# Attention's output projection in three products of high and low parts, with the context split by VectorE

## The chip, the cores and the metric

The kernel runs on one core of a Trainium2 chip. The metric is the device time of one execution in microseconds (us). The engines are TensorE (PE, with its weight loads as PEld), VectorE (DVE), ScalarE (ACT), GpSimd (POOL) and SyncE (SP), which here issues most of the DMAs.

## The reference, cut to what matters

The input is x of 2 x 2048 tokens with 256 features. Three residual steps follow each other:

```
x = x + 0.5 * ffn(layernorm(x))      # 8 experts, the best 2 per token, hidden width 176
x = x + attn(layernorm(x))
x = x + 0.5 * ffn(layernorm(x))      # the same expert weights
```

In attn a causal convolution of 3 taps makes q, k and v of 64 features each. The tokens are cut into 32 blocks of 128, 8 heads attend causally within each block, and the context ends in two products:

```
mha_out = einsum('bqhk,hko->bqo', ctx, wo) + bo     # 64 features
out = mha_out @ proj_w + proj_b                     # 64 -> 256 features
```

Everything is float32. The change touches only the last product.

## The kernel before, in words

The tokens are 32 tiles of 128 rows. The kernel has a first expert stage, the attention stage and a second expert stage; each engine's program is written out by hand in the same turns, and semaphores alone connect them.

The attention stage runs in turns i, one per tile (`turns`, from -8 to 36), as a software pipeline. In turn i TensorE does, in this order: the convolution of a pair of tiles, q and k in odd turns (L1602, 18 matmuls) and v in even turns (L1611, 12); the scores of tile i (L1618 and L1623); the transposes of tile i-1's probabilities (L1629); the transposes of a later tile's input and of an earlier tile's output (L1637, L1648); the router's logits (L1664); the **projection** of tile i-2 (`project`, L1590, into bank G); the context of tile i-1, already multiplied with wo (L1679, into bank F); the per-head q and k of tile i+1 (L1689); and the values of tile i (L1699, into bank F too). Since L1699 overwrites what L1679 left in F, it waits until VectorE has copied it: `after(pe, t["mhaT"], i)`.

VectorE's turn i has, around the change: the maxima of the scores (L1311), in even turns the low part of v (L1315), the residual addition of the projection's result (L1327, waits for `out`), its statistics (L1330, L1333), the copy of the logits (L1261), the **copy of the context** with its bias from F into mhaT (L1342, waits for `mha`, signals `mhaT`), the low part of a later tile's input (L1274), the sum of the experts' rows for a later tile (L968, twice), the reciprocals of the exponentials' sums (L1353), and the copy of q and k (L1266), for which the next turn's scores wait. After L1353 GpSimd multiplies the probabilities (L683) and then issues its gathers (L691) and scatters (L700), which are indirect DMAs. ScalarE copies the transposed probabilities (L804), and computes the exponentials (L813).

mhaT and proj_sb are float32. 64 features fill only half of the 128 partitions; with heads of even and odd number in the two halves, proj_w stands in both halves, and the product adds them. The expert stages and the convolution use float32r operands instead: a value is kept as a high part, rounded when it is written, and a low part, the difference, and three products (high by high, high by low, low by high) replace one float32 product.

proj_w is loaded by SyncE with the small constants, in `loads`.

Of the kernel before, what the change touches and what calls it, by code (L numbers as in the profile page):

```python
# [15 lines left out]
ALU = mybir.AluOpType  # L16
ACT = mybir.ActivationFunctionType
AX = mybir.AxisListType
F32 = mybir.dt.float32
F32R = mybir.dt.float32r  # L20
# [4 lines left out]
P = 128  # L25
BATCH, SEQ, D = 2, 2048, 256
TOKENS = BATCH * SEQ
TILES = TOKENS // P
DC = D // P
# [14 lines left out]
TAPS, W = 3, 64  # L44
# [52 lines left out]
def macaron_kernel(nc, x, conv_w, conv_b, wq, wk, wvT, wo, bq, bk, bo, proj_w, proj_b, gupT, dpT, rwT,  # L97
                   out, h_dram, y_dram):
    ctx = ExitStack()
    with ctx:  # L100
        def sb(name, shape, dt=F32):
            return ctx.enter_context(nc.sbuf_tensor(name, shape, dt))
# [28 lines left out]
        wo_sb = sb("wo_sb", [KD, NH, W])  # L131
# [3 lines left out]
        bo_sb = sb("bo_sb", [W, 1])  # L135
        cbv_sb = sb("cbv_sb", [W + 1, 1])
        wvo_sum = sb("wvo_sum", [W + 1, W])
        mha_bias = sb("mha_bias", [P, 1])
        proj_sb = sb("proj_sb", [P, D])
        projb_sb = sb("projb_sb", [33, D])  # L140
        projb_parts = sb("projb_parts", [P, D], F32R)
        ones_r = sb("ones_r", [P, P], F32R)
# [4 lines left out]
        minus_ident = sb("minus_ident", [P, P], F32R)  # L147
# [111 lines left out]
        G_USED = LG_AT + (POST + 2) * E  # L259
# [7 lines left out]
        prec = sb("prec", [P, 2, NH])  # L267
        mhaT = tile_oh[:, :, :].rearrange("p j n -> p (j n)").bitcast(F32)[:, 2 * P:3 * P]
        eps = sb("eps", [P, 1])
# [12 lines left out]
        F = pb("F", 1)  # L282
# [51 lines left out]
        def logits_of(t):  # L334
# [14 lines left out]
                 (bqk_sb[:, 1, :], bk.rearrange("a (m p) -> p (a m)", p=P)), (wvT_sb[:, :, :], wvT),  # L349
                 (wo_sb[:, :, :], wo), (bo_sb[:, :], bo), (proj_sb[0:W, :], proj_w), (proj_sb[W:2 * W, :], proj_w),  # L350
                 (projb_sb[0:1, :], proj_b), (projb_sb[32:33, :], proj_b)]
# [89 lines left out]
        def turns(turn):  # L441
            for i in range(FIRST_TURN, LAST_TURN):
                turn(i)
# [40 lines left out]
        def _(sp):  # L484
# [82 lines left out]
            sp.wait_ge(first["tokens"], 1)  # L567
            sp.dma_start(conv_sb, conv_w).then_inc(loaded, 16)
            store_y(0)
            fill_pads()  # L570
# [149 lines left out]
        def _(a):  # L720
# [42 lines left out]
            def attention():  # L763
# [71 lines left out]
                a.preload_act_table_set("natural_log_exp_and_others")  # L835
                a.wait_ge(loaded, 16 * (len(loads) + 1))
                a.activation(conv_qk[0][:, :, :], conv_sb_qk, ACT.Copy).then_inc(wprep, 1)
                for c in range(DC):
                    a.activation(conv_v_parts[0][:, c, :, :], conv_sb_v[:, c, :, :], ACT.Copy).then_inc(wprep, 1)
                a.activation(projb_all[:, D:], zeros[:, 0:G_USED - D], ACT.Copy)  # L840
                a.wait_ge(projb, 4)
                a.activation(projb_all[:, 0:D], G[:, 0:D], ACT.Copy).then_inc(projb, 1)
                a.wait_ge(projb, PROJB_AT)
# [88 lines left out]
        def _(v):  # L932
# [260 lines left out]
            def attention():  # L1193
# [93 lines left out]
                def turn(i):  # L1287
# [52 lines left out]
                    if there(i - 1):  # L1340
                        v.wait_ge(t["mha"], i)
                        v.tensor_tensor(mhaT[:, :], F[:, 0:P], mha_bias[:, 0:1].to_broadcast([P, P]), ALU.add  # L1342
                                        ).then_inc(t["mhaT"], 1)
                    if there(i + 3) and i >= 0:
# [50 lines left out]
                for c in range(DC):  # L1395
                    v.tensor_tensor(conv_v_parts[1][:, c, :, :], conv_sb_v[:, c, :, :],
                                    conv_v_parts[0][:, c, :, :].bitcast(F32), ALU.subtract).then_inc(wprep, 1)
                turns(turn)

# [9 lines left out]
        def _(pe):  # L1409
# [173 lines left out]
            def attention():  # L1583
# [4 lines left out]
                def project(b):  # L1588
                    pe.wait_ge(t["mhaT"], b + 1)
                    pe.matmul(G[:, 0:D], mhaT[:, :], proj_sb[:, :], start=False, stop=True, skip_group_check=True  # L1590
                              ).then_inc(t["out"], 1)

# [162 lines left out]
            keep_clock(F[:, :], 44)  # L1755
            pe.wait_ge(wprep, 7 + 2 * (1 + DC))
            attention()
# [46 lines left out]
```

## Time and profile before

| what | value |
|---|---|
| median of 3 runs (lowest, highest) | 794.87 us (792.56, 800.15) |
| the profiled execution: its own time | 796.36 us |
| its span, first to last instruction | 794.6 us |
| mean granted TensorE clock | 0.961 of full |
| busy: PE, PEld | 690.0 us (87%), 603.7 us |
| busy: DVE, ACT, POOL | 528.2 us (66%), 490.2 us (62%), 335.8 us (42%) |
| attention's tiles: context copies L1342, first to last start | 272.0 to 575.7 us, 32 of them |

The busy shares are means over stages with different limits. The expert stages, 605 to 750 us among them, keep TensorE almost wholly busy; within the attention stage this holds for some turns and not for others, so that stage has to be read turn by turn. A matmul's end is modelled by the profile: two matmuls overlap in the rows, and what one of them costs is the distance between starts.

### The profile page before, as it was taken

The numbers are of one execution on the slowest core, as the hardware profiler recorded it, in microseconds if no ns is written. First come the engines' busy times: TensorE is split into PE (matmuls) and PEld (weight loads), VectorE is DVE, ScalarE is ACT, GpSimd is POOL, SyncE is SP. The second block draws the span as 40 slices with busy tenths as digits, with TensorE's granted clock in tenths as the row PEclk, the third lists the DMA queues.
The fourth block names the chain that finished last, engine by engine and source line by source line (L and its number), as shares of the span: only waits on it lengthen the run. The fifth ranks groups of instructions, "written<-read, shape, count | busy, mean of one in ns | idle before, by whom it ended". The sixth has DMA issues, their size and how long they took to land. (4 is left out here: it accounts for less than half of the span.)

```text
span 794.6 us, 19426 instructions
## 1 busy us (share of the span) xinstructions
PE 690.0 (87%) x5468; PEld 603.7 (76%) x5468; DVE 528.2 (66%) x1813; ACT 490.2 (62%) x1734; POOL 335.8 (42%) x361
## 2 busy tenths in 40 slices
PE   3999799999999799998988889989635999999944
PEld 3976699999975688877767777778424999999833
DVE  6578566666656587786767576857664777777643
ACT  4766566666653587767766657767522666666633
POOL 5100544444416444455555545252551444444500
PEclk9999999999999999999999999999956999999979
DMA  9930354444422110011111111010124444444279
GB/s 313 279 110 13 124 147 141 143 130 127 128 82 85 39 41 28 28 41 55 55 55 48 61 41 48 22 55 2 61 91 117 132 128 125 128 131 126 83 288 346
DMA packets 57863, 83.40 MB, mean 105 GB/s; under 512 B 9520, under 2 KB 43827, under 8 KB 57780
## 3 DMA queue, kind: packets, MB, share of 16 engines
q1 hardware_dynamic: 44772, 47.63, 19.0%
q0 software_dynamic: 13008, 34.69, 14.0%
q8 instruction: 49, 0.80, 0.4%
q14 instruction: 34, 0.28, 0.1%
HBM read 45.77 MB, written 37.44 MB: 105 GB/s over the span
## 5 line engine op out<-in xcount | busy, mean ns | idle before, releaser
L1539 PE MATMUL CC<-w_hi,turned_parts 128*128 x568 | 172.5, 345 | 0.3 <-DVE turned_parts L1161 0.2
L655 POOL DMA_INDIRECT shared<-h_rows,tok_i x71 | 67.3, 948 | 119.0 <-issue 58.7
L667 POOL DMA_INDIRECT y_rows<-shared,y_dest x71 | 69.9, 985 | 88.7 <-DVE y_dest L1173 74.9
L683 POOL TENSOR_TENSOR pr<-pr,prec 128x1024 f32<-128x1024 f32 x31 | 58.8, 1895 | 112.2 <-DVE prec L1353 110.9
L1539 PEld LDWEIGHTS CC<-w_hi,turned_parts 128*128 128x128 f32 x568 | 103.8, 190 | 1.0 <-issue 0.9
L1539 PE MATMUL CC<-w_lo,turned_parts 128*128 x284 | 91.8, 323 | 0.0
L729 ACT ACTIVATE shared<-CC 128x176 f32<-128x176 f32 x142 | 45.1, 317 | 75.1 <-PE CC L1539 72.6
L813 ACT ACTIVATE pr<-SS,nmax 128x128 f32<-128x128 f32 x256 | 90.4, 400 | 0.8 <-issue 0.8
L700 POOL DMA_INDIRECT h_regions<-h_store,dest x64 | 63.1, 987 | 47.3 <-DVE dest L1256 27.3
L1156 DVE TENSOR_TENSOR shared<-shared,CC 128x176 f32<-128x176 f32 x142 | 48.0, 338 | 51.6 <-ACT shared L729 30.0
L691 POOL DMA_INDIRECT yg<-y_rows,slot_i x64 | 62.6, 977 | 34.9 <-DMA y_rows<-shared 15.5
L745 ACT ACTIVATE shared<-SS 128x256 f32<-128x256 f32 x142 | 54.6, 385 | 26.5 <-issue 15.5
L804 ACT ACTIVATE shared<-CC 128x512 f32<-128x512 f32 x64 | 34.7, 594 | 48.1 <-PE CC L1629 45.2
L813 ACT ACTIVATION_READ_ACCUMULATOR pr<-SS,nmax 128x1 f32 x256 | 61.8, 241 | 0.0
L1539 PEld LDWEIGHTS CC<-w_lo,turned_parts 128*128 128x128 f32 x284 | 54.1, 191 | 0.0
L1556 PE MATMUL SS<-w_hi,turned_parts 128*128 x142 | 51.8, 364 | 1.3 <-DVE turned_parts L1167 1.0
L1161 DVE TENSOR_TENSOR turned_parts<-A,turned_parts 128x256 fp32r<-128x256 f32 x72 | 30.6, 425 | 29.5 <-ACT turned_parts L734 28.5
L1311 DVE TENSOR_REDUCE nmax<-SS 128x8 f32<-128x1024 f32 x32 | 39.1, 1221 | 13.4 <-PE SS L1623 10.4
L1623 PEld LDWEIGHTS SS<-shared 64*128 64x128 f32 x512 | 31.1, 187 | 18.0 <-issue 9.7
L1161 DVE TENSOR_TENSOR turned_parts<-B,turned_parts 128x256 fp32r<-128x256 f32 x70 | 29.8, 425 | 21.0 <-ACT turned_parts L734 16.8
L1526 PE MATMUL A<-ident,shared 128*128 128x128 f32 x144 | 29.0, 283 | 16.1 <-DMA shared<-h_regions 12.6
L781 ACT ACTIVATE lnvar<-moments,eps 128x2 f32<-128x2 f32 x39 | 11.7, 300 | 48.9 <-DVE moments L1367 48.0
(318 smaller groups left out, 2055.4 us busy)
## 6 DMA issues: line engine op xcount, KB each, us to landing
shared<-h_regions SPq DMA_DIRECT2D x71, 129.0 KB
y_rows<-shared SPq DMA_DIRECT2D x71, 128.0 KB
w_lo<-y_rows SPq DMA_DIRECT2D x9, 512.0 KB, 8.4
x_sb<-in_x_dram SPq DMA_DIRECT2D x8, 512.0 KB, 8.3
out_dram<-x_sb SPq DMA_DIRECT2D x16, 256.0 KB, 5.7
w_hi<-y_rows SPq DMA_DIRECT2D x7, 512.0 KB, 11.9
w_lo<-in_gupT_dram SPq DMA_DIRECT2D x2, 1408.0 KB, 10.7
h_regions<-pad_rows SPq DMA_DIRECT2D x15, 129.0 KB
```

The source lines that it names most:

```text
L655: pool.indirect_dma_start(out=rows[:, s % RING, 0:D], out_offset=None, in_=h_dram[:, :], in_offset=bass.IndirectOffsetOnAxis(ap=tok_i[:, s ...
L667: pool.indirect_dma_start(out=y_dram[0:TOPK * TOKENS, :], out_offset=bass.IndirectOffsetOnAxis(ap=y_dest[:, s:s + 1], axis=0), in_=y_sb[:, ...
L683: pool.tensor_tensor(pr[:, q, :, :], pr[:, q, :, :], prec[:, q, :].unsqueeze(2).to_broadcast([P, NH, P]), ALU.mult).then_inc(t["norm"], 1)
L691: pool.indirect_dma_start(out=yg[:, q, k, :], out_offset=None, in_=y_dram[:, :], in_offset=bass.IndirectOffsetOnAxis(ap=slot_i[:, b, k:k + ...
L700: pool.indirect_dma_start(out=h_regions[:, :], out_offset=bass.IndirectOffsetOnAxis(ap=dest[:, q, k:k + 1], axis=0), in_=hr[:, q, :], in_o ...
L729: a.activation(gate[:, p, :], CC[:, 512 * p:512 * p + H], ACT.Silu).then_inc(r["silu"], 1)
L745: a.activation(y_sb[:, u % RING, :], SS[:, 512 * (u % 2):512 * (u % 2) + D], ACT.Copy).then_inc(r["y_sb"], 1)
L813: e = a.activation(pr[:, u % 2, h, :], SS[:, h * P:(h + 1) * P], ACT.Exp, bias=nmax[:, u % 2, h:h + 1], accum_out=psums[:, u % 2, h:h + 1])
L1156: v.tensor_tensor(hid[:, p, 0:H], gate[:, p, :], CC[:, 512 * p + H:512 * p + GU], ALU.mult).then_inc(r["hid"], 1)
L1161: v.tensor_tensor(rowsT_lo[:, p, :], (A, B)[p][:, 0:D], rowsT_hi[:, p, :].bitcast(F32), ALU.subtract).then_inc(r["rowsT_lo"], 1)
L1539: i = pe.matmul(CC[:, 512 * (u % 2):512 * (u % 2) + GU], rows_part[:, u % 2, c * P:(c + 1) * P], weights, start=(n == 1), stop=(n == 3 * DC))
L1556: pe.matmul(acc, hidA_hi[:, u % 2, :], w_hi[:, at_a], start=True, stop=False)
```

## The change

The context of a tile is written by VectorE twice: the high part (the sum of F and the bias, rounded to float32r) and then, after a wait for it, the low part (the same sum less the high part), which now gives the signal `mhaT`. They lie in two tiles that are no longer used by then. proj_w is split likewise, once: ScalarE writes the high part, VectorE the low part, between the first expert stage and the attention's turns. `project` becomes three float32r matmuls of 256 columns. proj_w's two loads move from `loads` to behind the load of the convolution's weights, in SyncE's queue.

```diff
-        proj_sb = sb("proj_sb", [P, D])
+        proj_lo = sb("proj_lo", [P, D], F32R)
...
-        mhaT = tile_oh[:, :, :].rearrange("p j n -> p (j n)").bitcast(F32)[:, 2 * P:3 * P]
+        mhaT_hi, mhaT_lo, proj_hi = minus_ident, ones_r, projb_parts
+        proj_sb = tile_oh[:, :, :].rearrange("p j n -> p (j n)").bitcast(F32)[:, 1536 + G_USED:1536 + G_USED + D]
...
-                 (wo_sb[:, :, :], wo), (bo_sb[:, :], bo), (proj_sb[0:W, :], proj_w), (proj_sb[W:2 * W, :], proj_w),
+                 (wo_sb[:, :, :], wo), (bo_sb[:, :], bo),
...
             sp.dma_start(conv_sb, conv_w).then_inc(loaded, 16)
+            for half in range(2):
+                sp.dma_start(proj_sb[W * half:W * (half + 1), :], proj_w).then_inc(loaded, 16)
             store_y(0)
...
-                a.wait_ge(loaded, 16 * (len(loads) + 1))
+                a.wait_ge(loaded, 16 * (len(loads) + 3))
...
                 a.wait_ge(projb, 4)
+                a.activation(proj_hi[:, :], proj_sb[:, :], ACT.Copy).then_inc(wprep, 1)
...
-                        v.tensor_tensor(mhaT[:, :], F[:, 0:P], mha_bias[:, 0:1].to_broadcast([P, P]), ALU.add
-                                        ).then_inc(t["mhaT"], 1)
+                        step(v.tensor_tensor(mhaT_hi[:, :], F[:, 0:P], mha_bias[:, 0:1].to_broadcast([P, P]), ALU.add))
+                        v.scalar_tensor_tensor(out=mhaT_lo[:, :], in0=F[:, 0:P], scalar=mha_bias[:, 0:1],
+                                               in1=mhaT_hi[:, :].bitcast(F32), op0=ALU.add, op1=ALU.subtract
+                                               ).then_inc(t["mhaT"], 1)
...
+                v.wait_ge(wprep, 7 + 2 * (1 + DC) + 1)
+                v.tensor_tensor(proj_lo[:, :], proj_sb[:, :], proj_hi[:, :].bitcast(F32), ALU.subtract
+                                ).then_inc(wprep, 1)
...
-                    pe.matmul(G[:, 0:D], mhaT[:, :], proj_sb[:, :], start=False, stop=True, skip_group_check=True
-                              ).then_inc(t["out"], 1)
+                    for n, (part, weights) in enumerate(((mhaT_hi, proj_hi), (mhaT_hi, proj_lo), (mhaT_lo, proj_hi))):
+                        x = pe.matmul(G[:, 0:D], part[:, :], weights[:, :], start=False, stop=(n == 2),
+                                      skip_group_check=True)
+                    x.then_inc(t["out"], 1)
...
-            pe.wait_ge(wprep, 7 + 2 * (1 + DC))
+            pe.wait_ge(wprep, 7 + 2 * (1 + DC) + 2)
```

VectorE's queue in an even turn of the attention stage, before (tile_oh holds mhaT) and then in the changed kernel (minus_ident and ones_r now hold the two parts):

```order
L1261 TENSOR_TENSOR lg<-G,zeros 128x8
L1342 TENSOR_TENSOR tile_oh<-F,mha_bias 128x128
L1274 TENSOR_TENSOR turned_parts<-A,turned_parts 128x2x128
L968 SCALAR_TENSOR_TENSOR x_sb<-yg,wts,x_sb 128x256 x2
L1353 RECIPROCAL prec<-psums 128x8
L1266 TENSOR_TENSOR shared<-CC,bqk_sb 128x1024
```

```order
L1265 TENSOR_TENSOR lg<-G,zeros 128x8
L1346 TENSOR_TENSOR minus_ident<-F,mha_bias 128x128
L1347 SCALAR_TENSOR_TENSOR ones_r<-F,mha_bias,minus_ident 128x128
L1278 TENSOR_TENSOR turned_parts<-A,turned_parts 128x2x128
L972 SCALAR_TENSOR_TENSOR x_sb<-yg,wts,x_sb 128x256 x2
L1359 RECIPROCAL prec<-psums 128x8
```

One instruction is new between the first write of the context and all that follows; nothing else changes its place.

## Rows read from the trace of the kernel before

**Rows 1.** Busy time by stretch: us, sums of each engine, PEclk, DMA share, GB/s.

```profile
275.00:300.00 25.00, 24.71 (x247) 20.51 (x246) 20.04 (x57) 19.76 (x77) 12.18 (x10) 1.00 0.12 33
400.00:450.00 50.00, 42.27 (x397) 35.29 (x398) 33.52 (x108) 33.23 (x129) 26.65 (x23) 0.97 0.15 49
```

**Rows 2.** Waits, 272 to 579 us: who waited for whom, us, times, longest.

```profile
DVE x_sb L1327 <- remote: 19.5, 9, 3.2
PE F L1699 <- issue: 16.9, 14, 5.1
...
DVE x_sb L1327 <- PE G L1590: 10.9, 11, 2.6
```

**Rows 3.** Timeline, a turn in which TensorE waits for the copy.

```profile
456.96 0.28 DVE L1342 TENSOR_TENSOR tile_oh<-F,mha_bias 128x128 f32<-128x128 f32 x1
...
457.34 0.47 PE L1699 MATMUL F<-wvo_hi,vst_hi 128*128 128x512 f32 x1 [1.05 <-issue]
```

**Rows 4.** Timeline, 441 to 445 us: projection, GpSimd's indirect DMAs, residual addition.

```profile
441.35 0.68 PE L1590 MATMUL G<-proj_sb,tile_oh 128*128 128x256 f32 x2
...
442.62 0.99 POOL L700 DMA_INDIRECT h_regions<-h_store,dest  x1 [0.30 <-issue]
...
444.51 0.42 DVE L1327 TENSOR_TENSOR x_sb<-x_sb,G 128x256 f32<-128x256 f32 x1 [3.14 <-remote]
```

**Rows 5.** Timeline, TensorE, a turn without idle time: start, us, instruction.

```profile
432.32 0.68 PE L1590 MATMUL G<-proj_sb,tile_oh 128*128 128x256 f32 x2
432.93 1.09 PE L1679 MATMUL F<-shared 128*64 128x128 f32 x16
```

**Rows 6.** Timeline, TensorE, the convolution's 18 matmuls: first, last, and what follows.

```profile
458.11 0.28 PE L1602 MATMUL B<-turned_parts,conv_qk_hi 128*128 128x256 f32 x1
...
460.13 0.28 PE L1602 MATMUL B<-turned_parts,conv_qk_hi 128*128 128x256 f32 x1
460.25 0.60 PE L1618 MATMUL SS<-mask_bf,ident_bf 128*128 128x512 bf16 x2
```

**Rows 7.** Groups by shape: xcount, busy us, mean ns, idle before.

```profile
L968 DVE SCALAR_TENSOR_TENSOR x_sb<-yg,wts,x_sb 128x256 f32<-128x256 f32 x44 | 21.2, 481 | 0.8
...
L1342 DVE TENSOR_TENSOR tile_oh<-F,mha_bias 128x128 f32<-128x128 f32 x26 | 7.4, 283 | 1.5 <-remote 1.2 <-PE F L1679 0.2
```

**Rows 8.** Instructions on bank G, one line: ns min/median/max, starts, shapes.

```profile
L1166 DVE TENSOR_TENSOR turned_parts<-G,turned_parts x70: 284/292/294, 89.9 to 751.5; 128x128 fp32r<-128x128 f32 x70
```

**Rows 9.** Timeline, VectorE: two instructions, the second waiting for the first.

```profile
319.32 0.16 DVE L1301 SCALAR_TENSOR_TENSOR at<-moments,at 128x2 f32<-128x2 f32 x1
319.51 0.16 DVE L1304 SCALAR_TENSOR_TENSOR arstd<-at,arstd 128x2 f32<-128x2 f32 x1
```

**Rows 10.** Timeline, VectorE, 313 to 315 us; a turn of TensorE without idle time.

```profile
313.34 0.42 DVE L1327 TENSOR_TENSOR x_sb<-x_sb,G 128x256 f32<-128x256 f32 x1 [0.50 <-PE G L1590]
313.91 0.43 DVE L1330 BATCH_NORM_STATS2 astats<-x_sb 128x6 f32<-128x256 f32 x1
...
314.63 0.28 DVE L1342 TENSOR_TENSOR tile_oh<-F,mha_bias 128x128 f32<-128x128 f32 x1
314.82 0.41 DVE L1274 TENSOR_TENSOR turned_parts<-A,turned_parts 128x256 fp32r<-128x256 f32 x1
```

**Rows 11.** Timeline, TensorE, 315 us: the values start after the context copy.

```profile
315.06 0.50 PE L1699 MATMUL F<-wvo_hi,vst_hi 128*128 128x512 f32 x1
```

**Rows 12.** Timeline, both engines, a turn with time to spare.

```profile
322.44 1.10 PE L1679 MATMUL F<-shared 128*64 128x128 f32 x16 [0.38 <-issue]
324.56 0.50 PE L1699 MATMUL F<-wvo_hi,vst_hi 128*128 128x512 f32 x1
...
323.58 0.29 DVE L1342 TENSOR_TENSOR tile_oh<-F,mha_bias 128x128 f32<-128x128 f32 x1
```

**Rows 13.** Timeline before the turns: a ScalarE copy; VectorE's last weight part, first wait.

```profile
235.00 0.36 ACT L842 ACTIVATE tile_oh<-G 128x256 f32<-128x256 f32 x1
...
235.84 0.62 DVE L1396 TENSOR_TENSOR conv_v<-tile_oh,conv_v 128x192 fp32r<-128x192 f32 x2
...
239.12 1.00 DVE L968 SCALAR_TENSOR_TENSOR x_sb<-yg,wts,x_sb 128x256 f32<-128x256 f32 x2 [2.66 <-DMA yg<-y_rows,slot_i]
```

**Rows 14.** Busy time by stretch, two drops of the granted clock; columns as rows 1.

```profile
446.40:449.90 3.50, 3.50 (x15) 3.17 (x14) 2.70 (x7) 1.08 (x3) 1.98 (x2) 0.51 0.02 5
470.30:473.80 3.50, 3.50 (x19) 2.73 (x16) 2.37 (x8) 2.15 (x7) 2.99 (x3) 0.51 0.00 0
```

**Rows 15.** Line L1342: count, ns min/median/max, first and last start.

```profile
L1342 DVE TENSOR_TENSOR tile_oh<-F,mha_bias x32: 257/281/292, 272.0 to 575.7; 128x128 f32<-128x128 f32 x32
```

## The prediction

> **What bounds the kernel now.** The expert stages keep TensorE busy and the change does not touch them, so I read the attention stage. First the busy time by stretch [rows 1]: early in the stage TensorE is busy 24.71 of 25.00 us, while between 400 and 450 us it is busy 42.27 of 50. In the early turns TensorE is the limit; later something else sets the pace, and VectorE (33.5 of 50) is not full either. So there a chain of waits is the limit. The list of waits [rows 2] names a link of it: 14 times TensorE stands idle in front of L1699, 16.9 us in sum. L1699 overwrites bank F and waits for the context copy L1342. The timeline of such a turn shows the link: L1342 starts at 456.96 and takes 0.28, TensorE's L1699 starts at 457.34, 0.10 us after the copy's end, and it had been idle for 1.05 us [rows 3]. The copy itself is late because the residual addition L1327 in front of it was. In the turn around 442 us the projection starts at 441.35 and takes 0.68, but the addition that waits for it starts at 444.51; GpSimd is issuing indirect DMAs until 443.61 [rows 4]. Nine such waits, 19.5 us, have no releaser in the view ("remote"), against 10.9 us in 11 waits that end with the projection [rows 2]. So in the slow turns the signal of the projection comes late for a reason other than the length of its matmuls. My reading is that the chain goes: addition, context copy, values and convolution, scores, exponentials, reciprocals, GpSimd, its DMAs, and again the addition. The new VectorE instruction is put inside this chain; the shorter projection lies mostly outside.
>
> **Part 1: the projection on TensorE, shorter.** Before, its two float32 passes start at 432.32 and the next instruction, without idle time, at 432.93: 0.61 us [rows 5]. Float32r matmuls of the same 256 columns, weights changing each time, come at (460.25 - 458.11) / 18 = 0.119 us [rows 6]. Three cost 0.36, so each tile saves 0.25 us of TensorE, 31 tiles 7.8 us if all of it counted. The result's signal comes earlier by a little less; I take 0.17 (0.25 less the longer tail of three overlapping ends, an estimate). These are bounds too: three loads of weights that could not overlap would make the saving zero.
>
> The Trainium skill (FP8 and Floating Point Precision, "TensorE Precision Notes") says that a true FP32 product takes four passes through the array. By that, four against three of 0.119 would save only 0.12 us per tile; the trace does not agree, with 0.61 us for the float32 product, five times 0.119.
>
> **Part 2: the context copy on VectorE, longer.** The high part costs what the copy did, 0.283 [rows 7]; written as float32r it has the form of a subtraction from bank G, 0.292 at the median [rows 8], no difference worth a term. Then comes the wait: a waiting neighbour starts 0.19 to 0.20 us after a start of 0.16 [rows 9], so it costs 0.035. The low part is a scalar_tensor_tensor of 128 columns, a form with no row of its own. The same operation takes 0.481 for 256 columns [rows 7] and 0.16 for two [rows 9]; half way between is 0.32. Sum: `mhaT` comes 0.36 us later after the copy's start, and what follows on VectorE moves by as much, since L1274 starts 0.19 after L1342 now [rows 10] and would start 0.315 + 0.24 after it. Bounds: 0.28 (the TensorTensor of 128 columns, [rows 8], with the wait hidden) and 0.63 (0.481 for the operation, 0.15 for the wait, as between L1327, 0.42 long, and L1330, 0.57 later, [rows 10]). I take 0.36, nearest to the same operation's own rows. Queued behind it on VectorE are the low part of the next input, the experts' sums, the reciprocals (GpSimd waits for them) and L1266 (the next scores wait for it).
>
> The Trainium skill (VectorE: DVE Perf Modes, "The DRAIN you can't avoid") holds that a semaphore between two VectorE instructions costs nothing extra. By that the delay would be 0.32; here L1274 starts before L1342 has ended [rows 10], and the waiting pair has a gap [rows 9], so the wait has a price.
>
> **Part 3: what it does to the turns.** In the 14 turns where L1699 waits for the copy, the chain grows by 0.36: 14 x 0.36 = **+5.0 us**. TensorE's saving is worth nothing there: it only makes TensorE idle earlier. In 3 of these the addition waited visibly for the projection's end; 3 x 0.17 = **-0.5**. The other 17 turns are of two kinds. In the turn at 313 us the copy ends at 314.91 and L1699 starts at 315.06 [rows 10, 11]: with the 0.10 us that a signal takes, 0.05 is to spare. The later copy then takes TensorE's saving and 0.14 to 0.31 more; I take 0.2, for half of them: 8 x 0.2 = **+1.6**. In the turn at 323 us the copy ends at 323.87 and L1699 starts at 324.56, 0.59 to spare; but L1679 had waited 0.38 for ScalarE anyway [rows 12], so a shorter projection in front of it gains nothing: **0**, for the other nine. Sum **+6.1 us**.
>
> **Part 4: the rest.** ScalarE's high part of proj_w (0.36, as its copy of 256 columns) and VectorE's low part (0.42, as L1327) fall before the turns. VectorE ends its last weight part at 236.46 and then idles 2.66 us for a gather [rows 13]; if that cover were gone, they would cost 0.4 to 0.8 us, once. The two loads, 64 x 256 numbers each, pass in SyncE's queue in front of the first expert stage's stores, which wait for expert results anyway, and have that whole stage to land. Bank G, the tiles reused and the tail after the last turn: 0.
>
> **The sum.** 796.36 + 6.1 = 802.5 for the profiled execution, which lies 1.5 us over the median of the three runs. From the median, 794.87 + 6.1 = **801.0 us**, 0.8% slower. The bounds of the copy's price alone give 14 x 0.28 - 0.5 + 0.6 = +4 and 14 x 0.63 - 0.5 + 8 x 0.5 = +12.3, that is 799 to 807. A change of under 1% (7.9 us, 786.9 to 802.8) cannot be told from none with the spread of 7.6 us that three runs showed.
>
> **The rivals.**
> *The gain arrives (not slower).* TensorE is the limit where it is 99% busy [rows 1], and if the extra VectorE time falls into its waits for the projection (10.9 us in 11, [rows 2]), some 16 turns (half, an estimate: those without idle time in front of L1679) gain 0.25: 794.87 - 4 = 791; all 31 would give 787. For it: [rows 1, 5]. Against: in [rows 10, 11] the margin is 0.05 us, and the slow turns wait for exactly the instruction that grows. It decides where more than 0.2 us is to spare behind the copy. Chance 0.2.
> *VectorE binds in every turn (slower).* Everything behind the copy moves by 0.36, the q and k copy with it, for which the scores wait; then the turns with time to spare pay as well: 31 x 0.36 = +11.2, 806; at the upper price 814. For it: 33.5 of 50 us busy, and waits on both sides of the chain. Against: in [rows 12] the margin is 0.59. Chance 0.2.
> *More drops of the clock.* The granted clock fell to 0.51, its lower level of 1.2 GHz, for 3.4 us at 446 and at 470 us, each time after turns with idle time in front of L1699 [rows 14, 3]; TensorE does half its work there, so a drop costs at most 1.7 us. Two more, on top of my forecast: 804.4. Two fewer: 797.6. Chance of two more 0.1.
> The Trainium skill (TensorE: Matmul & The Clock Gate, "HAM oscillation") says that idle gaps make the clock fall again; the drops stand behind such gaps here, so the trace agrees.
> *It does not do what it says:* three float32r matmuls with their loads cost as much as the float32 pair. Then the nearly tight turns pay the full 0.36: +8 x 0.16 = 1.3 over the forecast, 802.3. Against: [rows 6]. Chance 0.05, counted with the forecast's range.
>
> **Chances.** Forecast 0.45, and 0.05 for the last rival; around 801 with a few us either way, two thirds of it is under 802.8. Gain 0.2: mostly within 1%, 0.05 beyond. VectorE in every turn 0.2 and clock 0.1: nearly all slower. Together: faster by over 1% 0.05, within 1% 0.52, slower by over 1% 0.43. The range takes the gain at its likely size and the slower rival at its lower price: 791 to 807.
>
> **What would show it.** Right: two rows for the context, 0.28 and about 0.32 us, starts 0.32 apart; L1699's counterpart starting about 0.7 after the first; three matmuls 0.12 apart; more than 14 waits and more than 16.9 us in front of the values. Wrong: the low part under 0.25 or above 0.45; TensorE's idle time in front of the values no larger, and the mean distance of two tiles, now (575.7 - 272.0) / 31 = 9.80 us [rows 15], shorter instead of 0.2 longer. What would overturn it all is a change of the lateness of projection signals, 19.5 us now [rows 2], since no part of my sum moves that.

## The result and the profile after

| | before | after |
|---|---|---|
| median of 4 runs (lowest, highest) | 796.73 us (792.56, 800.15) | 810.01 us (806.89, 813.68) |
| ratio of after to before, 95% interval | | 1.0149 [1.0106, 1.0193] |
| profiled execution: its time, span | 796.36, 794.6 us | 812.69, 811.0 us |
| mean granted TensorE clock | 0.961 | 0.936 |
| first to last context copy, per tile | 303.6 us, 9.80 us | 317.1 us, 10.23 us |

The kernel became 1.5% slower, twice what was forecast (0.8%), and the time lies above the range. In the two profiled spans the difference is 16.4 us: 13.4 between the first and the last context copy, 0.6 ahead of them (they start at 272.6 instead of 272.0 us) and 2.4 behind them. So the loss is in the attention turns, as forecast, 0.43 us for each of 31 tile distances instead of 0.2. In this pair of executions a good part of it can be the clock; see the end of this section. A few executions of some kernels fell in a much slower state of the chip (up to 3582 us); the ratios leave them out, while the medians of "split late" and "signal alone" on the slow chip hold two and one of them.

The context's two instructions in the profile after, by line (count, ns min/median/max, first and last start), answer to [rows 15]:

```profile
L1346 DVE TENSOR_TENSOR minus_ident<-F,mha_bias x32: 256/281/292, 272.6 to 589.7; 128x128 fp32r<-128x128 f32 x32
...
L1347 DVE SCALAR_TENSOR_TENSOR ones_r<-F,mha_bias,minus_ident x32: 350/351/352, 272.9 to 590.0; 128x128 fp32r<-128x128 f32 x32
```

The high part costs what the copy did, the low part 0.351 us where 0.32 was forecast. A turn in which TensorE waits for them, first VectorE's rows (start, us, instruction, idle time before it); the next row of the values is below. This answers to [rows 3]:

```profile
454.45 0.42 DVE L1331 TENSOR_TENSOR x_sb<-x_sb,G 128x256 f32<-128x256 f32 x1 [3.74 <-remote]
455.01 0.43 DVE L1334 BATCH_NORM_STATS2 astats<-x_sb 128x6 f32<-128x256 f32 x1
455.59 0.18 DVE L1337 BATCH_NORM_AGGREGATE moments<-astats 128x2 f32<-128x6 f32 x1
455.69 0.13 DVE L1265 TENSOR_TENSOR lg<-G,zeros 128x8 f32<-128x8 f32 x1
455.74 0.28 DVE L1346 TENSOR_TENSOR minus_ident<-F,mha_bias 128x128 fp32r<-128x128 f32 x1
456.05 0.35 DVE L1347 SCALAR_TENSOR_TENSOR ones_r<-F,mha_bias,minus_ident 128x128 fp32r<-128x128 f32 x1
456.32 0.41 DVE L1278 TENSOR_TENSOR turned_parts<-A,turned_parts 128x256 fp32r<-128x256 f32 x1
...
456.50 0.47 PE L1710 MATMUL F<-wvo_hi,vst_hi 128*128 128x512 f32 x1 [1.59 <-issue]
```

L1347 starts 0.31 after L1346, so the wait between them costs 0.03 as forecast. The values (L1710) start 0.76 after the high part, against 0.38 before [rows 3], and L1278 starts 0.58 after it, against 0.19 [rows 10]. Both the values and the queue are 0.38 to 0.39 us later, counted from the start of the first write.

The turn that was costed at nothing because 0.59 us was to spare [rows 12] looks like this in the profile after, TensorE and VectorE:

```profile
322.73 0.37 PE L1600 MATMUL G<-projb_parts,minus_ident 128*128 128x256 f32 x1
322.93 0.28 PE L1600 MATMUL G<-proj_lo,minus_ident 128*128 128x256 f32 x1
323.05 0.28 PE L1600 MATMUL G<-projb_parts,ones_r 128*128 128x256 f32 x1
323.26 1.09 PE L1690 MATMUL F<-shared 128*64 128x128 f32 x16
324.29 1.16 PE L1700 MATMUL CC<-tile_oh,wqk_sb 64*128 64x128 f32 x16
325.43 0.47 PE L1710 MATMUL F<-wvo_hi,vst_hi 128*128 128x512 f32 x1
...
324.66 0.28 DVE L1346 TENSOR_TENSOR minus_ident<-F,mha_bias 128x128 fp32r<-128x128 f32 x1
324.98 0.35 DVE L1347 SCALAR_TENSOR_TENSOR ones_r<-F,mha_bias,minus_ident 128x128 fp32r<-128x128 f32 x1
```

The low part ends at 325.33 and the values start at 325.43, the 0.10 us of a signal later: in this turn nothing is to spare any more, and the 0.38 that L1679 had waited for ScalarE is gone as well. The three products start 0.20, 0.12 and 0.21 us apart, 0.53 from the first to what follows, against 0.61 for the float32 pair [rows 5]. They save 0.08 us and not 0.25. Where float32r products follow each other the distance is 0.119 [rows 6]; here the first one, behind float32 matmuls, and the last one, before them, each take about 0.09 more.

The list of waits after, 272 to 592 us (who waited for whom, us, times, longest), answers to [rows 2]:

```profile
DVE x_sb L1331 <- remote: 27.0, 10, 3.7
...
PE F L1710 <- issue: 26.3, 22, 5.6
...
DVE x_sb L1331 <- PE G L1600: 6.8, 11, 1.2
```

TensorE now stands idle in front of the values 22 times for 26.3 us, where it was 14 times for 16.9. Taken turn by turn, the values start 0.10 us behind the end of the instruction that signals in 29 of 31 turns, before in 15. This counts the turns that the signal touches, not what they pay: on another chip, where the change costs only 0.39% (below), the same count is 29 against 7. The wait for the projection fell from 10.9 to 6.8 us, and the late signals ("remote") rose from 19.5 to 27.0. Busy times by stretch after (us, sums of PE, PEld, DVE, ACT, POOL, granted clock, DMA share, GB/s), two as in [rows 1] and the attention stage's core:

```profile
275.00:300.00 25.00, 24.03 (x246) 20.29 (x245) 20.27 (x58) 19.39 (x77) 11.49 (x9) 1.00 0.12 33
400.00:450.00 50.00, 44.36 (x397) 37.26 (x396) 34.14 (x111) 30.59 (x113) 26.46 (x24) 0.90 0.15 46
265.00:540.00 275.00, 244.72 (x2346) 206.66 (x2345) 195.84 (x624) 184.76 (x710) 135.84 (x113) 0.96 0.14 43
582.00:630.00 48.00, 22.84 (x109) 19.14 (x110) 25.75 (x132) 11.51 (x32) 15.31 (x16) 0.51 0.30 86
```

Early TensorE has become less busy, 24.03 of 25 instead of 24.71. In the core, VectorE is busy 195.84 of 275 us: 71%, still far from full.

The clock differs too. The span between the first and the last context copy, before and then after, and the stretch of the profile after in which the clock falls before the last copy:

```profile
272.00:575.70 303.70, 272.08 (x2608) 225.17 (x2608) 215.57 (x708) 209.35 (x806) 149.37 (x124) 0.98 0.13 42
```

```profile
272.60:589.70 317.10, 278.28 (x2639) 234.25 (x2639) 226.06 (x739) 210.44 (x808) 149.52 (x125) 0.95 0.13 40
580.90:589.70 8.80, 7.34 (x39) 6.13 (x39) 6.24 (x33) 3.87 (x10) 2.15 (x3) 0.50 0.05 17
```

By the clock's records TensorE is at its lower level (1.2 GHz) for 13.7 us of this span before and for 32.7 us after, and is busy for 13.7 and 30.4 of them. If it does half its work there, as the prediction has it, the 16.7 us more cost at most 8.4 of the 13.4 us.

### The profile page after: what moved, and what is told of

Same layout as the page of the kernel before. It is cut to its first block, busy times and chain, and to the rows that moved or that the text cites. A ratio compares the mean times of both kernels' runs of the same rounds, so it can differ in the third digit from the quotient of the medians.

```text
span 811.0 us, 19524 instructions
## 1 busy us (share of the span) xinstructions
PE 701.4 (86%) x5500; PEld 618.5 (76%) x5500; DVE 539.8 (67%) x1846; ACT 491.5 (61%) x1735; POOL 334.7 (41%) x361
## 3 DMA queue, kind: packets, MB, share of 16 engines
q0 software_dynamic: 13008, 34.69, 13.7%
## 4 chain that ended last, share of the span: by engine, by line
PE 75%; issue 8%; DVE 6%; DMA 5%; ACT 3%; SPq 2%; another core or an unknown queue 1%; POOL 1%; DVEq 0%; POOLq 0%; ACTq 0%
PE CC L1548 17%; PE CC L1640 4%; PE SS L1634 4%; PE CC L1700 4%; PE B L1613 4%; PE F L1710 4%; PE F L1690 3%; PE B L1622 3%; PE A L1535 2%; PE SS L1565 2%; PE SS L1566 2%; PE SS L1567 2%; PE SS L1568 2%; PE SS L1569 2%; PE B L1535 2%
## 5 line engine op out<-in xcount | busy, mean ns | idle before, releaser
L1548 PE MATMUL CC<-w_hi,turned_parts 128*128 x568 | 174.8, 349 | 0.2 <-DVE turned_parts L1165 0.2
L1700 PE MATMUL CC<-tile_oh,wqk_sb 64*128 64x128 f32 x512 | 41.5, 287 | 5.0 <-issue 4.6
L1535 PE MATMUL A<-ident,shared 128*128 128x128 f32 x144 | 29.3, 285 | 16.9 <-DMA shared<-h_regions 13.1
## 6 DMA issues: line engine op xcount, KB each, us to landing
w_hi<-y_rows SPq DMA_DIRECT2D x7, 512.0 KB, 12.1
```

Of the source, the lines that this page charges most:

```text
L1535: i = pe.transpose((A, B)[s % 2][:, c * P:(c + 1) * P], rows[:, s % RING, c * P:(c + 1) * P], ident[:, :])
L1548: i = pe.matmul(CC[:, 512 * (u % 2):512 * (u % 2) + GU], rows_part[:, u % 2, c * P:(c + 1) * P], weights, start=(n == 1), stop=(n == 3 * DC))
L1700: x = pe.matmul(CC[:, 512 * n + m * P:512 * n + (m + 1) * P], wqk_sb[W * n:W * (n + 1), m * P:(m + 1) * P], qk[W * n:W * (n + 1), q, :], s ...
```

## The experiments

All medians are of kernels timed in turns with the kernel before on the same chip. Two sorts of chip came up: on one the kernel before takes 797 us, on the other 758. I call them the slow and the fast chip; each sort came up on more than one chip. Short names in what follows: the **signal** is `mhaT`, for which TensorE waits; the **queue** is what stands behind the copy on VectorE. Letters in an expectation are explained in it or in the ones ahead of it.

| experiment | chip | median, us | before there | ratio [95%] | per tile, us |
|---|---|---|---|---|---|
| (before, profiled) | slow | | | | 9.80 |
| low part alone | slow | 805.89 | 797.45 | 1.0134 [1.0064, 1.0205] | 10.00 |
| products alone | slow | 799.05 | 797.45 | 1.0021 [0.9993, 1.0048] | 10.00 |
| low part twice | slow | 820.07 | 797.45 | 1.0284 [1.0229, 1.0339] | 10.52 |
| split late | slow | 804.06 | 797.45 | 1.0075 [1.0043, 1.0106] | 9.98 |
| signal alone | slow | 803.04 | 797.33 | 1.0080 [1.0054, 1.0106] | 9.96 |
| queue alone | slow | 801.76 | 797.33 | 1.0050 [1.0022, 1.0079] | 9.95 |
| copy first (before) | slow | 802.12 | 797.33 | 1.0058 [1.0027, 1.0089] | 9.81 |
| before again | fast | 758.60 | 758.74 | 0.9997 [0.9976, 1.0018] | 8.75 |
| after again | fast | 761.87 | 758.74 | 1.0039 [1.0022, 1.0056] | 8.85 |
| queue alone | fast | 761.74 | 758.74 | 1.0045 [1.0024, 1.0067] | 8.90 |
| signal alone | fast | 758.70 | 758.74 | 1.0002 [0.9988, 1.0017] | 8.77 |
| copy first (before) | fast | 761.53 | 757.71 | 1.0046 [1.0032, 1.0061] | 8.86 |
| copy first (after) | fast | 771.05 | 757.71 | 1.0159 [1.0132, 1.0186] | 9.10 |
| fillers (after) | fast | 769.41 | 757.71 | 1.0154 [1.0128, 1.0180] | 9.10 |
| split on GpSimd | fast | 763.04 | 757.71 | 1.0075 [1.0051, 1.0099] | 8.79 |

"Per tile" is from one profiled execution, first to last context copy by 31; the verdicts go by the ratios. The distances on the slow chip carry the clock with them. "Products alone" shows it: its ratio is 1.002, but the execution that was profiled is the slowest of its ten (803.75 us), with 10.00 us per tile. Between its first and last copy TensorE was at the lower clock for 28.7 us (before: 13.7) and busy for 26.7 of them, which would cost up to 6.5 us; its span there is 6.3 us longer than before's. So up to 0.2 us per tile can come without any change on VectorE.

**1. The low part alone, in the kernel before.** The same added instruction, written to a spare tile, gives the signal; the projection stays float32.

```diff
-v.tensor_tensor(mhaT, F, bias, add).then_inc(t["mhaT"], 1)
+step(v.tensor_tensor(mhaT, F, bias, add))
+v.scalar_tensor_tensor(out=ones_r, in0=F, scalar=bias, in1=mhaT, op0=add, op1=subtract).then_inc(t["mhaT"], 1)
```

> The kernel before (float32 projection, one copy used) with the change's low-part instruction added behind the context copy: it computes the low part into a spare tile, nobody reads it, and it alone gives the signal mhaT. Theory A (the signal mhaT comes 0.39 us later per tile and nearly every turn waits for it): 31 x 0.39 = 12 us over before plus about 1 for a slower clock, and within 3 us of the changed kernel, since the shorter projection was worth at most 31 x 0.08 = 2.5. Theory B (the float32r products of the change themselves cost time, in the array or by the clock): under 5 us over before. As predicted blind (14 turns pay 0.36): +5.

Measured 1.0134, against 1.0149 for the whole change. These ratios agree within their intervals (0.6 to 2.0% and 1.1 to 1.9%). The waits of its profiled execution, which at 802.45 us is one of the two short ones of four (median 805.89), 272 to 592 us:

```profile
PEld F L1701 <- issue: 29.5, 23, 5.7
PE F L1701 <- issue: 24.4, 21, 5.5
DVE x_sb L1327 <- PE G L1592: 17.8, 18, 2.3
...
DVE x_sb L1327 <- remote: 9.9, 5, 3.7
```

The 21 waits and 24.4 us in front of the values are those of the profile after (22 and 26.3). "Remote" is at 9.9 us, half of before's 19.5. The profile puts such a wait sometimes to a late signal and sometimes to the projection, so the two lines are to be read together: 30.4 us before, 27.7 here, 33.8 after. The waits of the addition thus do not grow with the added instruction alone.

**2. The products alone.** The change with one copy only: the low part of the context is left out, and the third product takes the high part a second time.

```diff
-step(v.tensor_tensor(mhaT_hi, F, bias, add))
-v.scalar_tensor_tensor(out=mhaT_lo, ...).then_inc(t["mhaT"], 1)
+v.tensor_tensor(mhaT_hi, F, bias, add).then_inc(t["mhaT"], 1)
...
-for ... in enumerate(((mhaT_hi, proj_hi), (mhaT_hi, proj_lo), (mhaT_lo, proj_hi))):
+for ... in enumerate(((mhaT_hi, proj_hi), (mhaT_hi, proj_lo), (mhaT_hi, proj_hi))):
```

> The changed kernel with one copy of the context only: the low part of the context is left out, and the third product uses the high part again, so TensorE's work is that of the change and VectorE's that of before (this kernel leaves the context's low part out of the result). Theory A: VectorE's queue is as before, so the time is too; TensorE saves 0.08 us a tile by the rows of the changed kernel, worth 0 to 2.5 us: between 3 us under before and before. Theory B: 5 us or more over before. My blind figure of 0.25 us per tile would show as 4 to 8 us under before.

Measured 1.0021, with 1 inside the interval. The products gain nothing in time: at 0.08 us per tile they could give 31 x 0.08 = 2.5 us (0.3%) at most, and at the 0.25 of the forecast 7.8 us; the interval (-0.6 to +3.8 us) excludes both in full. The granted clock of these ten runs was lower than that of the kernel before beside them (medians 0.948 and 0.955), so a small gain may lie under it; this was not separated.

**3. The low part twice.** In the change the low part is computed a second time before the signal.

```diff
+step(v.scalar_tensor_tensor(out=mhaT_lo, in0=F, scalar=bias, in1=mhaT_hi, op0=add, op1=subtract))
 v.scalar_tensor_tensor(out=mhaT_lo, ...).then_inc(t["mhaT"], 1)
```

> The changed kernel with the low part computed twice in a row, the second giving the signal: another 0.385 us per turn between the copy's start and mhaT. Theory A: all turns but one or two pay it already, so 31 x 0.385 = 12 us over the changed kernel, 24 to 26 over before; the mean distance of two tiles grows by 0.385. If the changed kernel's extra time came from more drops of the clock, not from the delay itself: under 5 us over the changed kernel.

Measured 1.0284. Over the change this is 1.35% more, 10.8 us by the ratios or 0.35 us for each of 31 distances; the second low part with its wait is 0.351 + 0.035 = 0.39 long. The first one cost 0.34 per distance (10.7 us by experiment 1). The intervals are wide: 0.17 to 0.53 us for either. In the profiled executions the span between first and last copy grows by 9.1 us over the change's, 0.29 per distance, at much the same time at the lower clock (34.1 and 32.7 us). So the second low part is paid in most turns; for the first one no pair of executions at the same clock is on record.

**4. The split late.** VectorE copies the context in float32 and frees F, as before; the high and the low part are made from that copy at the end of the turn.

```diff
+v.tensor_tensor(mhaT, F, bias, add).then_inc(low_act, 1)
...
+step(v.tensor_copy(mhaT_hi, mhaT))
+v.tensor_tensor(mhaT_lo, mhaT, mhaT_hi, subtract).then_inc(t["mhaT"], 1)
```

> The changed kernel with the context copied once in float32, which alone releases bank F, and split from that copy into high and low part on VectorE at the end of the turn, behind the statistics (two instructions, some 0.5 us, and one copy more than the change). Theory A1 (what costs is the lateness of the signal that releases bank F): the signal comes as early as before, so within 3 us of before, although VectorE works more than in the changed kernel. Theory A2 (what costs is VectorE's time, wherever it stands in the turn, since its queue closes the loop): 31 x 0.5 = 15 us over before. Halfway, 5 to 8 over, if the turns with idle time on VectorE absorb it and the others do not.

Measured 1.0075. Between first and last copy its profiled execution is 5.7 us longer than before's, with about the same time at the lower clock (15.0 and 13.7 us). VectorE's rows of this kernel, grouped by shape:

```profile
L1375 DVE CAST minus_ident<-tile_oh 128x128 fp32r<-128x128 f32 x32 | 14.3, 446 | 0.0
L1376 DVE TENSOR_TENSOR ones_r<-tile_oh,minus_ident 128x128 fp32r<-128x128 f32 x32 | 11.0, 344 | 1.1
```

VectorE does 0.79 us more per turn here, twice the change's addition, at about half the change's cost by the ratios. So it is not VectorE's sum of work alone that counts but where in the turn it lies. It is still slower than before.

**5 and 6. Signal and queue apart.** The added instruction delays two things at once. "Queue alone" puts an instruction of its kind behind the signal, in the kernel before. "Signal alone" gives the signal by a write of one column (0.06 us) behind the next VectorE instruction, so the queue hardly grows.

```diff
 v.tensor_tensor(mhaT, F, bias, add).then_inc(t["mhaT"], 1)
+v.wait_ge(t["mhaT"], i)                                       # queue alone
+v.scalar_tensor_tensor(out=ones_r, in0=mhaT, scalar=bias, in1=mhaT, op0=add, op1=subtract)
```

```diff
-v.tensor_tensor(mhaT, F, bias, add).then_inc(t["mhaT"], 1)    # signal alone
+v.tensor_tensor(mhaT, F, bias, add)
 ...low part of the next input...
+v.memset(number_off[:, 0:1], 0.0).then_inc(t["mhaT"], 1)
```

Both were run on the fast chip first, beside the two kernels unchanged:

> The kernel before, unchanged, to have its profile from the same chip as the next three: the last four kernels ran on a chip where the kernel before takes 758 us, 40 us less than on the chip of its own profile. If this chip is the fast one, TensorE is busy over 97% of the attention stage and waits for the context copy in under 7 turns.

> The changed kernel, unchanged. Ratio to before 1.015 as on the first chip; with fillers it was 1.0154 on the second, so if fillers neither help nor cost, the same here. If the copy's place in TensorE's wait is all that matters, a chip without late signals would show under 1.008.

> The kernel before with a scalar_tensor_tensor of 128 columns behind the context copy, on the copy in SBUF: the signal mhaT is given first, as before, and only what follows on VectorE comes some 0.4 us later. Theory A (the signal is what costs): within 2 us of before. Theory C (VectorE's queue closes the loop): 8 to 12 us over, as much as with the low part alone. Half of each: 4 to 7.

> The kernel before with the signal mhaT given by a one-element memset behind the next VectorE instruction, so that it comes some 0.35 us later while VectorE's queue grows by 0.06 us only. Theory A: 8 to 12 us over before on a chip with late signals of TensorE, 3 to 8 on one without. Theory C: within 2 us of before.

There the whole change costs only 0.39%, which is 3.0 us or 0.10 us per tile out of 0.39 added; the longer queue costs as much (0.45%), and the late signal nothing (0.02%). The clock hardly enters here: between the first and the last copy it is at the lower level for 3.4 us in both profiles. Then on the slow chip:

> The same kernel as the one with VectorE's queue alone made longer, on another chip if the draw gives one. If this is a chip with late signals of TensorE (kernel before near 797 us): theory D (there the loop runs through VectorE, GpSimd and the late signals, and every instruction in VectorE's queue lies in it) expects 7 to 12 us over before; theory A (only the signal mhaT counts) within 2 us. On a chip without them (near 758): 3 us, as measured.

> The same kernel as the one with the signal alone late, on another chip if the draw gives one. On a chip with late signals: theory D expects 0 to 4 us over before, for the turns in which the values wait; theory A 8 to 12. On one without: 0, as measured.

Here the late signal costs 0.80% (0.54 to 1.06) and the longer queue 0.50% (0.22 to 0.79), so which of the two costs more is not settled. Their sum, 1.3%, fits the low part alone (1.34%, 0.64 to 2.05), but the intervals leave room. That the late signal costs time here and none on the fast chip is clear of the noise. VectorE and TensorE in one turn of "signal alone" on the slow chip:

```profile
333.22 0.28 DVE L1350 TENSOR_TENSOR tile_oh<-F,mha_bias 128x128 f32<-128x128 f32 x1
333.41 0.41 DVE L1274 TENSOR_TENSOR turned_parts<-A,turned_parts 128x256 fp32r<-128x256 f32 x1
333.78 0.06 DVE L1283 MEMSET number_off<- 128x1 f32 x1
...
333.95 0.47 PE L1708 MATMUL F<-wvo_hi,vst_hi 128*128 128x512 f32 x1 [0.23 <-issue]
```

The values start 0.73 after the copy instead of 0.38, while L1274 keeps its distance of 0.19: the edit moved the signal and left the queue, as it should. The waits of "signal alone" and then "queue alone" on the slow chip, 265 to 590 us:

```profile
PE F L1708 <- issue: 25.5, 21, 5.2
```

```profile
PE F L1702 <- issue: 19.7, 16, 5.2
```

The late signal brings the number of waits to that of the change (21 against 22); the longer queue leaves it near that of before (16 against 14) and costs through what is behind it instead.

**7. The context copied first.** The copy, or both parts, is put right behind the residual addition, ahead of its statistics and the copy of the logits.

```diff
 v.sem_inc(t["res"], 1)
+if there(i - 1):
+    v.wait_ge(t["mha"], i)
+    ...the copy, or both parts, with the signal...
 st.did(v.bn_stats(astats[:, 1, :], x_tile(b)))
```

> The kernel before with one instruction moved: the context copy stands directly behind the residual addition, ahead of the statistics and the copy of the logits. Theory A (the wait of L1699 for the copy sets the pace of the slow turns): the signal comes up to 0.7 us earlier there (1.28 us between the starts of addition and copy now, 0.55 then); TensorE's wait in front of L1699 in the 14 turns, 16.9 us without its share of the last turn 11.8, shrinks by up to 0.7 each: 4 to 8 us under before. Theory C (VectorE's queue as a whole closes the loop, and no single signal does): within 2 us of before.

> The changed kernel with both parts of the context made directly behind the residual addition. Theory A: the signal comes 0.7 us earlier, more than the 0.39 the change added: at or under before (-4 to +2 us), that is 10 to 16 us under the changed kernel. Theory C: VectorE's 0.385 us per turn stay in its queue: 5 to 8 us under the changed kernel at most, still over before.

> The kernel before with the context copy directly behind the residual addition, on another chip if the draw gives one. On a chip with late signals: theory A expects 4 to 8 us under before, since the signal comes 0.7 us earlier; theory D from 2 under to 4 over, as VectorE's queue keeps its length and what follows the copy waits for the context. On one without: 3.5 over, as measured.

Slower on both sorts of chip in the kernel before (0.46%, 0.58%), and 1.59% over before with both parts, on a fast chip where the change itself costs 0.39%. On the slow chip the one profiled execution shows no longer distance of tiles (9.81 us against 9.80), so where its 0.58% lies is not shown. A reason that fits is that an earlier place in the queue is not an earlier start: on the slow chip the copy now waits itself for TensorE's context, and holds up the statistics and the logits behind it (265 to 590 us):

```profile
DVE tile_oh L1332 <- PE F L1681: 9.7, 16, 1.1
```

**8. Fillers against the clock's drops.** Three idle matmuls of 512 bfloat16 columns before the wait for the signal, in the change.

```diff
+for _ in range(3):
+    pe.matmul(B, ident_bf, mask_4, start=True, stop=True)
 after(pe, t["mhaT"], i)
```

> The changed kernel with three filler matmuls of 512 bf16 columns (0.21 us each, results not used) into bank B, ahead of the wait for mhaT, so that TensorE is busy where it stood idle. If drops of the granted clock carry the extra time (changed kernel: seven drops between 265 and 580 us, 24 us at half clock, before: four): the clock holds and the time falls by 3 to 6 us. Theory A: the fillers lie in idle time of 0.5 to 1.7 us in most turns and cost up to 0.6 us in the tight ones: 0 to 5 us over the changed kernel, whatever the clock does.

Inconclusive: the run fell on a fast chip, where TensorE is nearly always busy, and the kernel with fillers is 1.5% over before where the change alone is 0.4%, so the fillers cost about 1.1%. It says nothing on the slow chip's clock, where the question arose; this test was not run there.

**9. The split on GpSimd.** VectorE makes one float32 copy and GpSimd the two parts.

```diff
+v.tensor_tensor(mhaT, F, bias, add).then_inc(low_act, 1)
...
+steps.did(pool.tensor_copy(mhaT_hi, mhaT))
+pool.tensor_tensor(mhaT_lo, mhaT, mhaT_hi, subtract).then_inc(t["mhaT"], 1)
```

> The changed kernel with VectorE's part as before (one float32 copy, which releases bank F), and both parts made from it by GpSimd, ahead of its wait for the reciprocals, where it idles 4 us a turn. Signal and VectorE's queue are as before, the three products as in the change: by theory A and C alike within 2 us of the kernel with the products alone, 797 to 800. If GpSimd's additional time pushes its gathers: up to 10 us over before.

Measured 1.0075 on a fast chip, where the change costs 0.39%. It is no cure. The two instructions take 294 and 490 ns at the median, in front of the multiplication of the probabilities; that this is what costs is argued, not shown. No version beat the kernel before on either chip, so none is proposed.

## Why the prediction was wrong

**The place held.** The added VectorE instruction between the context and its signal makes the kernel slower (experiment 1 alone gives 1.34 of 1.49%), the products bring nothing measurable (experiment 2), and all else (proj_w's parts, the loads, bank G) shows at most the 0.6 us by which the turns start later.

**Part 1, mis-sized.** The projection saves 0.08 us and not 0.25. The row at [rows 6] was measured within a run of float32r matmuls, and here three of them stand between float32 ones. The last rival, that it does not do what it says, was two thirds true. This moved the sum little: the -0.5 did not come, and that is all that Part 1 gave to it.

**Part 2, nearly right.** 0.39 us instead of 0.36: 0.351 for the low part, 0.035 for the wait. In 14 turns that is +0.4.

**Part 3, the first step that failed.** It let 14 turns pay in full, 8 pay 0.2, and 9 nothing, because in a turn like [rows 12] 0.59 us was to spare. It read the slack of one turn as if that turn stood alone. In the profile after, the same turn has nothing to spare, and the values wait for the signal in 29 of 31 turns. The explanation offered is that the turns are a ring, where what one turn gives its successor late the successor has no longer to spare; this is argued. On the fast chip the signal is as tight (29 of 31), the late signal costs nothing there, and the change costs 0.10 us per tile, so a tight signal is not yet a price. How much of Part 3's 6.1 us is missing is therefore not told by the count of tight turns.

**The clock, the second step that failed.** The sum put it at nothing, and the rival of two more drops had a chance of 0.1. Between the first and the last copy the lower clock lasts 32.7 us after against 13.7 before: six stretches, one of them twice as long (410 to 417 us), against four, and then 8.8 us of the long stretch that begins at 580.9, while before it begins at 579.6, behind the last copy. By halved work that is up to 8.4 of the 13.4 us, which leaves at least 5.0 for the delay. The other executions after point the same way: 806.89 us at a mean clock of 0.950, 807.33 at 0.944, 812.69 at 0.936, 813.68 at 0.940. In 41 executions of the kernel before on other slow chips the median is 0.955, and in them 0.001 of clock goes with 0.4 to 0.5 us. By that, an estimate, some 5 to 6 us of the change's loss go with its lower clock. This does not tell cause from effect, since longer waits may themselves bring the drops: four of the six stretches after (from 365.8, 389.7, 468.2 and 543.3 us) begin within 1.5 us of the end of a wait of 1.4 to 1.7 us in front of the values. Nor is the lower clock bound to the added instruction: "products alone" had 28.7 us of it in its slowest execution.

**How the two share the miss stays open.** The rival "VectorE binds in every turn", at 0.2, comes nearest in number: 31 x 0.39 = 12.1 us, against a measured 11.9 (8.4 to 15.4, from the ratio and its interval), and 796.73 + 12.1 = 808.8 against a median of 810.0. But Part 3 as it stood, with 0.39 for 0.36, is 6.5 us, and with 5 to 6 us for the clock this gives 11.5 to 12.5 as well. The runs do not choose between them: experiment 3 shows the second low part paid in most turns at an equal clock, not the first, and experiment 8 showed nothing for the slow chip. The name of the rival is not right in any case. VectorE does not bind by its work (71% busy, and experiment 4 adds twice as much for about half the cost). Two things follow the copy, the values through the signal and the next scores through the queue, and each costs time by itself on the slow chip (0.8% and 0.5%).

Behind the last copy the clock stays low until 628.6 us, where before it was low from 579.6 to 610.3; the 2.4 us behind the last copy fall there, and that they come from the clock is argued, not shown.

**What the prediction said would overturn it,** a change of the late signals, did not show itself as the cause. The addition's waits, "remote" and projection together, are 30.4 us before and 33.8 after, and 27.7 in experiment 1. Of TensorE's signals between 265 and 580 us about as many are late before as after (last section).

## What to carry to other kernels

Where engines hand work round in a ring, don't take the spare time that a single turn shows for time that the next turns have as well: here the turn with 0.59 us to spare had none after the change. What the added 0.39 us costs per turn depends on what else is late: 0.10 us on one sort of chip, 0.34 to 0.38 by the ratios on the other, the clock's share included. An instruction in front of a signal delays two parties, the waiter on the other engine and its own queue; test each alone. Before two profiled executions are compared, compare their clocks: here "products alone" ran 0.2 us per tile longer at a lower clock with no such loss in its median. A matmul format's price is to be read from a place with the same neighbours: three products between others in another format cost 0.53 us where three of a long run would cost 0.36.

## What the runs showed of the hardware

**Two sorts of chip.** The same kernel took 797 us on some chips and 758 on others, at nearly the same mean granted clock (0.961 and 0.962 in the profiled executions, 0.955 and 0.962 at the median of all). By tile it is 9.80 against 8.75 us. Busy times of the kernel before, 265 to 540 us, on the slow chip:

```profile
265.00:540.00 275.00, 249.96 (x2405) 207.69 (x2405) 194.89 (x619) 191.16 (x735) 138.25 (x114) 0.98 0.14 43
```

and on the fast chip, with the waits of the residual addition and the values:

```profile
265.00:540.00 275.00, 266.01 (x2628) 221.47 (x2629) 218.44 (x716) 211.21 (x816) 151.82 (x127) 0.99 0.15 48
```

```profile
DVE x_sb L1327 <- PE G L1590: 12.7, 19, 1.1
...
PE F L1699 <- issue: 4.0, 7, 2.0
```

TensorE is busy 97% of the stretch on the fast chip and 91% on the slow one. The wait called "remote" [rows 2] doesn't exist there. In the semaphore records of the slow chip some 100 to 120 of TensorE's signals between 265 and 580 us, by how updates and matmuls are paired, come over 0.3 us after the modelled end of their matmul, before and after alike; on the fast chip none does. GpSimd's indirect DMAs [rows 4] go with it: they run for 31% of that time, but 74 of 100 such matmuls ended during one of them, and 24 of 150 others did. Why some chips do this stays open. The two sorts of chip differ in what the change costs, 1.5% on the one and 0.4% on the other, where a late `mhaT` is free; that the late signals are the reason is likely and not shown, since nothing was run that changes them alone.

**Neighbours of a matmul.** In the projection, the first float32r product behind float32 matmuls and the last one in front of them take about 0.09 us more each than among their own kind (0.20, 0.12, 0.21 against 0.119 us; the same in the median of the turns without idle time). Whether the format or the shapes of the neighbours do it was not tested.

**A copy in SBUF of uneven length.** VectorE's cast of 128 x 128 from SBUF (experiment 4) took 220 to 1056 ns, 446 on average; the subtraction behind it 291 to 365, 344 on average. What makes the difference was not tested.
